# One program for the second layer's norm, routing and refinement, with three blocks of masks made inside the refinement

## The chip, the cores and the metric

The kernel runs on one core of a Trainium2 chip. The metric is the device time of one execution in microseconds. TensorE (PE) multiplies, ScalarE (ACT) evaluates functions and copies, VectorE (DVE) does elementwise work, GpSimd (POOL) helps, and SyncE (SP) starts transfers. Each runs its own instruction list in order and waits for the others by semaphores.

## The reference, cut to what matters

Two layers work on 2 x 1024 tokens of width 128. Only the last part, `_L1_ffn_ref`, is touched. It starts from a layernorm of the residual `x`:

```
logits = gelu(xf @ w_r1 + b_r1) @ w_r2 + b_r2          # 8 experts
top_p, top_i = top_k(softmax(logits), 2); top_p /= sum(top_p)
for _ in range(2):                                      # NUM_ITER
    ctx = concat(integrated, v)
    shared = inl(gelu(ctx @ w_s1 + b_s1) @ w_s2 + b_s2)
    routed = sum over the 2 picks c of top_p[c] * inl(gelu(ctx @ w1[i_c] + b1[i_c]) @ w2[i_c] + b2[i_c])
    x_next, v = sw * shared + (1 - sw) * routed
    integrated += sigmoid(gelu(x_next @ w_h1 + b_h1) @ w_h2 + b_h2) * (gelu(x_next @ w_f1 + b_f1) @ w_f2 + b_f2) * iw
# inl: alpha, beta, gate = sigmoid, softplus, sigmoid of the three thirds of the control;
#      v' = alpha*v - beta*(x - mu); x' = x + 0.1*gate*v'
```

## The kernel before

Tokens lie along the free dimension: `x` and `hn` are 128 features x 2048 tokens, in 4 blocks of 512 (`BLK`), or 16 tiles of 128. The kernel is a chain of programs. Each `with nc.Block()` gives every engine its list, and at its end all engines meet at a barrier. After the latent attention, `experts_of_layer1` runs these, one after the other:

- a program that starts the loads of the expert weights (`ew2`, `eb2_rows`), halves two biases, and lets POOL clear 85 used semaphores (`clear_stale`);
- `split_bias`: seven DVE instructions split the expert bias into bf16 parts (`eb2w`);
- `normalise`: center product, squares, means over 128 partitions, square root and reciprocal, spreading of the 2048 inverse norms (L189), and the product into `hn`;
- `route`: the router's two products (one `products` program each), the choice of two experts for each token (DVE, L2473 to L2506, with one Exp on ACT), the turn of the choice from tokens along partitions to tokens along the free dimension (`picks`, 27 rows), and the spreading of `picks` to `masks` and `mixw`: for each block 8 masks (2 picks x 4 pairs of experts) and 2 weights, 40 products in all, which DVE and ACT copy out of PSUM;
- `refine`: eight units `u` (4 blocks, twice). `hidden(u)` is 5 products with a Gelu each on two banks; `mask(u)` multiplies the hidden values with the masks on DVE; `control(u, comp, s)` makes part `comp` (1 beta, 2 gate, 0 alpha) for pick 0, pick 1 or the shared expert. For a pick that is one product with `eb2w` (L2658) and four with `ew2` (L2661), fp32, two passes each. `halt_*` are the products of the halting head. The order on each engine is written out by hand. `log_exp` changes ACT's table for the softplus, `hidden` changes it back.

`products` gives each step a PSUM bank in turn out of eight, and PE waits for the engine that took the step eight places earlier.

Of the kernel before, what the change touches and what calls it, by code (L numbers as in the profile page):

```python
# [5 lines left out]
F32 = mybir.dt.float32  # L6
# [6 lines left out]
D = 128  # L13
# [19 lines left out]
        "b_s2_0", "b_s2_1", "b_s2_2", "stat_eps"] + [f"eb1_{p}" for p in range(4)] + [f"part{i}" for i in range(3)] + ["eps_rms", "eps_ln"]  # L33
# [101 lines left out]


def normalise(k, tag, src, ncols, outs, groups=1, eps=1e-5, centre=None):


    nc = k.nc  # L140
    nb, nt = ncols // BLK, ncols // TILE
    width = nt * groups
    with ExitStack() as ctx:
        sq = k.sb(f"{tag}_sq", [128, ncols], ctx=ctx)
        ve = k.sb(f"{tag}_ve", [128, width], ctx=ctx)
        sd = k.sb(f"{tag}_sd", [128, width], ctx=ctx)
        r = k.sb(f"{tag}_r", [128, width], ctx=ctx)
        t = k.sb(f"{tag}_t", [128, width], ctx=ctx)

        rx = r if groups == 1 else k.sb(f"{tag}_rx", [128, width, HD], ctx=ctx)  # L150
        centred = k.sem(f"{tag}_centred")
        src_ready = k.sem(f"{tag}_src_ready")
        squared = k.sem(f"{tag}_squared")
        stat_done = k.sem(f"{tag}_stat_done")
        var_ready = k.sem(f"{tag}_var_ready")
        sd_ready = k.sem(f"{tag}_sd_ready")
        r_ready = k.sem(f"{tag}_r_ready")
        spread = k.sem(f"{tag}_spread")
        scaled = k.sem(f"{tag}_scaled")
        own = k.sem(f"{tag}_own")  # L160
        stat = k.bank[6][:, 0:width]
        mean = k.m("mean128") if groups == 1 else k.m("mean8")
        per = BLK // TILE
        with nc.Block() as block:
            @block.tensor
            def _(pe):
                if centre is not None:
                    for b in range(nb):
                        nc.tensor.matmul(k.bank[b][:, :], k.m("center"), centre[:, sl(b)], start=True, stop=True)\
                            .then_inc(centred, 1)  # L170
                for b in range(nb):
                    pe.wait_ge(squared, b + 1)
                    for j in range(b * per, (b + 1) * per):
                        last = nc.tensor.matmul(stat[:, j * groups:(j + 1) * groups], sq[:, sl(j, TILE)], mean,
                                                start=True, stop=True)
                last.then_inc(stat_done, 1)
                pe.wait_ge(r_ready, 1)
                for b in range(nb):
                    if b >= 2:
                        pe.wait_ge(scaled, (b - 1) * len(outs))  # L180
                    elif centre is not None:
                        pe.wait_ge(src_ready, nb)
                    for j in range(per):
                        jt = b * per + j
                        if groups == 1:
                            lhs = r[:, jt:jt + 1].to_broadcast([128, 128])
                        else:
                            lhs = rx[:, jt * groups:(jt + 1) * groups, :].rearrange("p g d -> p (g d)")
                        last = nc.tensor.matmul(k.bank[4 + b % 2][:, sl(j, TILE)], lhs, k.m("ident"),  # L189
                                                start=True, stop=True)  # L190
                    last.then_inc(spread, 1)

            @block.scalar
            def _(act):
                for b in range(nb):
                    if centre is not None:
                        act.wait_ge(src_ready, b + 1)
                    nc.scalar.activation(sq[:, sl(b)], src[:, sl(b)], ACT.Square).then_inc(squared, 1)
                act.wait_ge(var_ready, 1)
                nc.scalar.activation(sd[:, :], ve[:, :], ACT.Sqrt).then_inc(sd_ready, 1)  # L200

            @block.vector
            def _(dve):
                link = linker(dve, own)
                if centre is not None:
                    for b in range(nb):
                        dve.wait_ge(centred, b + 1)
                        nc.vector.tensor_copy(src[:, sl(b)], k.bank[b][:, :]).then_inc(src_ready, 1)
                dve.wait_ge(stat_done, 1)
                nc.vector.tensor_scalar_add(ve[:, :], stat, eps).then_inc(var_ready, 1)  # L210
                dve.wait_ge(sd_ready, 1)
                link(nc.vector.reciprocal(r[:, :], sd[:, :]))

                link(nc.vector.tensor_tensor(t[:, :], r[:, :], r[:, :], ALU.mult))
                link(nc.vector.tensor_tensor(t[:, :], t[:, :], ve[:, :], ALU.mult))
                link(nc.vector.tensor_scalar(t[:, :], t[:, :], -0.5, 1.5, ALU.mult, ALU.add))
# [2896 lines left out]
```

## Time and profile before

| | |
|---|---|
| median of 3 runs | 2122.79 us (2122.67 to 2124.22) |
| profiled execution | 2126.78 us, its span 2125.0 us |
| busy, share of the span | PE 84%, DVE 72%, ACT 65%, POOL 32% |
| share of the chain that ended last | PE 13% (of it L2661 7%), DVE 1%, ACT 1% |
| last part begins | about 1742.2 us into the span, the refinement at 1809.7 us |

Busy time is a share of the whole span, so it averages stages with different limits. The granted clock (PEclk) is a share of 2.4 GHz: 1.00 is 2.4 GHz and 0.50 is 1.2 GHz. In rows of the trace, `L12` is a line of the kernel, `xN` the number of instructions merged, and the bracket behind a row the idle time of the engine before it and what ended it. An fp32 product shows two matmuls. PEld is the loading of weights.

### The profile page before, as it was taken

Reading aid. Unit: us, or ns where it says so; the run is one execution under the profiler, and the core shown is the slowest. Engines: PE = TensorE matmul, PEld = TensorE weight load, DVE = VectorE, ACT = ScalarE, POOL = GpSimd, SP = SyncE. Lnnn points to the kernel's source line nnn. Section 1 sums busy time; section 2 is a strip of 40 time slices with the busy share of each in tenths; the row PEclk is TensorE's granted clock in tenths of the full one; section 3 lists DMA queues with packets and bytes.
Section 4 is the critical chain, followed back from the end, with each engine's and each line's share of the span. In section 5 each row is a group of like instructions: output and inputs, shape, how many; then the busy total and the mean of one; then the engine's idle time right before and its main releaser. Section 6 shows DMA issues by size and latency. Waiting matters only on the chain. (4 is left out here: it accounts for less than half of the span.)

```text
span 2125.0 us, 31609 instructions
## 1 busy us (share of the span) xinstructions
PE 1775.6 (84%) x10320; PEld 730.3 (34%) x10320; DVE 1534.3 (72%) x1538; ACT 1388.8 (65%) x2914; POOL 678.3 (32%) x384
## 2 busy tenths in 40 slices
PE   6799999997787666667666679989999977999996
PEld 1233333333333333333333234334444434333332
DVE  5788888844799999999999854456666625456446
ACT  2277777775899999999999724235555544344343
POOL 1000000001799999999999820010000000000000
PEclk8599999999688878887888799869999986999997
DMA  4111111001666665555555320412323100000000
GB/s 157 44 27 30 32 32 27 13 2 34 216 207 207 202 201 200 197 196 199 201 199 202 119 80 10 95 45 45 56 39 56 23 17 1 0 0 0 0 5 15
DMA packets 57886, 182.39 MB, mean 86 GB/s; under 512 B 8487, under 2 KB 11842, under 8 KB 56239
## 3 DMA queue, kind: packets, MB, share of 16 engines
q1 hardware_dynamic: 57487, 180.46, 28.0%
q8 instruction: 70, 1.15, 0.2%
q10 hardware_dynamic: 288, 0.45, 0.1%
q14 instruction: 41, 0.34, 0.1%
HBM read 160.60 MB, written 7.21 MB: 79 GB/s over the span
## 5 line engine op out<-in xcount | busy, mean ns | idle before, releaser
L648 DVE TENSOR_REDUCE attn_mx<-banks 128x1 f32<-128x1024 f32 (+7 forms) x512 | 501.5, 989 | 161.4 <-PE banks L455 102.2
L600 ACT ACTIVATE attn_probs<-banks 128x512 f32<-128x512 f32 (+3 forms) x896 | 446.5, 550 | 256.6 <-PE banks L485 151.6
L1722 POOL TENSOR_TENSOR hc<-st,ct 128x1024 f32<-128x1024 f32 x256 | 598.5, 2364 | 46.7 <-DVE st L1680 46.6
L1680 DVE TENSOR_TENSOR_SCAN st<-da,banks 128x1024 f32<-128x1024 f32 x256 | 566.6, 2269 | 19.7 <-DVE banks L1672 13.4
L1645 ACT ACTIVATE ut<-b_turned,x_now 128x128 f32<-128x128 f32 x1280 | 389.6, 387 | 3.1 <-PE banks L1538 1.4
L1637 ACT ACTIVATE da<-dt,a_now 128x1024 f32<-128x1024 f32 x256 | 284.1, 1136 | 10.6 <-DVE st L1680 8.9
L1538 PE MATMUL banks<-mats,ut 128*128 128x128 f32 x1280 | 234.5, 328 | 56.6 <-DVE st L1680 36.0
L505 PE MATMUL banks<-attn_probs,attn_vst 128*32 128x256 f32 (+3 forms) x3584 | 273.2, 376 | 4.1 <-ACT attn_osb L591 3.8
L485 PE MATMUL banks<-attn_qa,attn_ka 75*128 75x512 bf16 (+3 forms) x896 | 271.8, 372 | 4.2 <-DMA attn_qa<-attn_mrow 1.9
L1561 PE MATMUL banks<-hc,onecol 128*32 128x512 f32 x1024 | 178.9, 778 | 100.6 <-POOL onecol L1713 91.0
L1538 PEld LDWEIGHTS banks<-mats,ut 128*128 128x128 f32 x1280 | 183.1, 163 | 170.2 <-ACT ut L1645 101.2
L453 PE MATMUL banks<-attn_ka,attn_qa 64*128 64x512 bf16 (+3 forms) x512 | 198.9, 389 | 31.9 <-DVE attn_mx L648 27.2
L2661 PE MATMUL banks<-hid_m,ew 128*128 128x512 f32 x320 | 150.3, 613 | 0.0
L453 PE MATMUL banks<-attn_ku,attn_qu 64*128 64x512 bf16 (+3 forms) x384 | 145.3, 379 | 0.0
L1421 POOL MEMSET dr<- 1x2048 f32 x1 | 1.8, 1797 | 418.5 <-POOLq L355 418.5
L485 PEld LDWEIGHTS banks<-attn_qa,attn_ka 75*128 75x128 bf16 x896 | 80.8, 98 | 132.2 <-ACT attn_probs L600 56.9
L453 PEld LDWEIGHTS banks<-attn_ka,attn_qa 64*128 64x128 bf16 x512 | 47.8, 94 | 205.6 <-issue 130.4
L505 PEld LDWEIGHTS banks<-attn_probs,attn_vst 128*32 128x32 f32 x3584 | 73.4, 109 | 101.8 <-issue 90.8
L1551 PE MATMUL banks<-xparts,sel 96*128 96x512 bf16 x160 | 65.4, 501 | 44.7 <-DVE st L1680 43.4
L1672 DVE TENSOR_TENSOR banks<-bt,banks 128x1024 f32<-128x1024 f32 x80 | 96.6, 1207 | 1.7 <-PE banks L1551 1.7
L2661 PEld LDWEIGHTS banks<-hid_m,ew 128*128 128x128 f32 x320 | 58.4, 192 | 71.0 <-issue 71.0
L2845 DVE TENSOR_TENSOR beta<-beta,beta_raw 128x1536 f32<-128x1536 f32 x8 | 14.1, 1758 | 84.0 <-ACT beta L2773 84.0
(430 smaller groups left out, 1765.5 us busy)
## 6 DMA issues: line engine op xcount, KB each, us to landing
dt<-dt_rows SPq DMA_DIRECT2D x256, 512.0 KB, 4.1
attn_qa<-q_lin SPq DMA_DIRECT2D x144, 64.0 KB
attn_qu<-attn_qa SPq DMA_DIRECT2D x16, 512.0 KB, 4.2
attn_ka<-k_lin SPq DMA_DIRECT2D x72, 64.0 KB
moe_w<-in_moe_w SPq DMA_DIRECT2D x2, 2048.0 KB, 10.4
mats<-in_mats SPq DMA_DIRECT2D x1, 2876.5 KB, 15.2
attn_ku<-attn_ka SPq DMA_DIRECT2D x8, 256.0 KB, 5.0
q_lin<-qparts SPq DMA_DIRECT2D x6, 256.0 KB
```

Of the source, the lines that this page charges most:

```text
L453: ins = nc.tensor.matmul(out[:, lo:hi], lhs, rhs, start=True, stop=not diag)
L485: ins = nc.tensor.matmul(out[:, c0:BLK], ka[i % RING][0:KROWS, kj(j), sl(kt, TILE)], qa[i % RING][0:KROWS, j, qb * BLK + c0:(qb + 1) * BLK ...
L505: last = nc.tensor.matmul(out_acc[32 * j:32 * j + 32, cols], vstage[:, kt, kj(j), :], probs[(kt_slot + j // 2) % 4][:, j % 2, cols],  star ...
L600: nc.scalar.activation(probs[s % 4][:, jj, c0:BLK], scores_exp[jj][:, c0:BLK], ACT.Exp, scale=scale).then_inc(probs_ready, 1)
L648: nc.vector.reduce_max(mx[:, qt, j:j + 1], scores_max[n % 2][:, 0:w], AX.X)\
L1538: ins = nc.tensor.transpose(pair[:, i // 4, sl(i % 4, TILE)], buf[:, i, :], k.m("ident"))
L1561: last = nc.tensor.matmul(y_bank[h][32 * g:32 * g + 32, :], col[jp % 2][:, :], hc[(4 * jp + g) % 8][:, sl(h)], start=False, stop=False, sk ...
L1637: nc.scalar.activation(da[n % 4][:, :], dt[n % 4][:, :], ACT.Exp, scale=a_now[:, g, jp:jp + 1])\
L1645: nc.scalar.activation(ut[TURNED.index(n) % 2][:, i, :], b_turned[:, 8 * b + i, :], ACT.Copy, scale=x_now[:, i, g, jp:jp + 1]).then_inc(ut ...
L1680: nc.vector.tensor_tensor_scan(st[n % 4][:, :], da[n % 4][:, :], pair[:, :, :].rearrange("p h t -> p (h t)"), 0.0, ALU.mult, ALU.add).then ...
L1722: nc.gpsimd.tensor_tensor(hc[n % 8][:, :], st[n % 4][:, :], ct[:, b * SEQ:(b + 1) * SEQ], ALU.mult)\
L2661: last = nc.tensor.matmul(out[:, :], w2[:, p, comp * D:(comp + 1) * D], hid_m[u % 2][:, s, p, :], start=False, stop=p == PAIRS - 1)
```

## The change

All of that becomes one program, with one barrier before it and one behind it:

- The norm takes its guess from Ln and Exp (ACT, one table) and one refining step (DVE), squares are read from PSUM, and the kept copies of the centered values lie in buffers of the refinement.
- The router writes its four blocks to four row groups of one bank, so that one Gelu covers them. `hidden(0)` is issued around the logits: 2 of its 5 products before, 3 behind.
- The constants (`ident_b`, `sel`, `sel_w`, `half_b`, `hb2`) and the split bias are made on POOL, behind its clearing of semaphores (`tables` counts them: 4 before the first turn, 14 before the first control product).
- Only block 0 has its choice turned and its masks made ahead of the refinement, on six banks. Blocks 1 to 3 are 36 ring steps (per block 2 turns and 10 masks or weights), on banks 6 and 7 alone. 2 are issued ahead of the first control product, the other 34 between the control products of units 0 and 1, and ACT alone copies them out. Halting products, which use the same banks, wait for the last ring copy.

The pieces stand in this order: where the ring steps lie (`(u, comp, s)`: first step, count), PE's ring, PE's control product, PE's halting product of units 0 and 7, PE's start, ACT's start and unit, DVE's mask.

```
+    in_ring = {(0, 1, 0): (2, 4), (0, 1, 1): (6, 4), (0, 1, 2): (10, 4), (0, 2, 0): (14, 4), (0, 2, 1): (18, 4),
+               (0, 2, 2): (22, 4), (1, 1, 0): (26, 2), (1, 1, 1): (28, 2), (1, 1, 2): (30, 2), (1, 2, 0): (32, 2),
+               (1, 2, 1): (34, 2)}
...
+            def ring(first, count):
+                for n in range(first, first + count):
+                    b, r = 1 + n // RING, n % RING
+                    if n >= 2:
+                        pe.wait_ge(ring_copied, n - 1)
+                    if r == 2:
+                        pe.wait_ge(ring_copied, n)
+                    out = k.bank[6 + n % 2]
+                    ins = turn(out, b, r) if r < 2 else widen(out, b, r - 2)
+                    ins.then_inc(ring_made, 1)
...
                 for p in range(PAIRS):
                     last = nc.tensor.matmul(out[:, :], w2[:, p, comp * D:(comp + 1) * D], hid_m[u % 2][:, s, p, :],
                                             start=False, stop=p == PAIRS - 1)
-                last.then_inc(made, 1)
+                    if p == PAIRS - 1:
+                        last.then_inc(made, 1)
+                    if count == PAIRS:
+                        ring(first + p, 1)
+                    elif count and p % 2:
+                        ring(first + p // 2, 1)
...
+                else:
+                    pe.wait_ge(ring_copied, RINGS)
...
-            hidden(0)
+            normalise()
+            router()
+            hidden(0, 0, 2)
+            logits()
+            hidden(0, 2)
+            first_block()
+            ring(0, 2)
...
+            normalise()
+            router()
             hidden(0)
+            nc.scalar.preload_act_table_set("natural_log_exp_and_others")
+            act.wait_ge(diff_ready, 1)
+            nc.scalar.activation(best[:, :, 1], best[:, :, 1], ACT.Exp).then_inc(exps_ready, 1)
+            first_block()
+            ring(0, 2)
             for u in range(NU):
...
+                for s in (0, 1, SHARED):
+                    ring(*in_ring.get((u, 1, s), (0, 0)))
                 if u + 1 < NU:
                     hidden(u + 1)
-                gates(u, 0)
-                gates(u, 1)
+                for s in (0, 1):
+                    ring(*in_ring.get((u, 2, s), (0, 0)))
+                    gates(u, s)
...
             def mask(u):
+                if u == 0:
+                    dve.wait_ge(masks_dve, PAIRS + 1)
+                    dve.wait_ge(masks_act, PAIRS + 1)
+                elif u < NBLK:
+                    dve.wait_ge(ring_copied, RING * u)
```

On PE, the start of the refinement before: `hid_m` are the masked hidden values, `ew` the expert weights, `hn` the normalized input of `hidden`.

```order
L733 MATMUL banks_7<-picks,route_sel_w 128x512
L725 UNCONDITIONAL_BRANCH
L2626 UNCONDITIONAL_BRANCH
L2641 MATMUL banks_1<-hn,mats 128x512 x4
L2641 MATMUL banks_1<-hn,mats 64x512
L2658 MATMUL banks_3<-picks,eb2w 128x512
L2661 MATMUL banks_3<-hid_m,ew 128x512 x4
L2658 MATMUL banks_3<-picks,eb2w 128x512
L2661 MATMUL banks_3<-hid_m,ew 128x512 x4
L2654 MATMUL banks_5<-hid_s,mats 128x512
L2641 MATMUL banks_1<-hn,mats 128x512 x4
```

The same place in the changed kernel, from the last masks of block 0 on (`route_ident` with `route_tok` is a turn, `route_sel` with `picks` a mask, in its own numbering of lines):

```order
L2438 MATMUL banks_5<-picks,route_sel_w 128x512
L2430 MATMUL banks_7<-route_ident,route_tok 27x128 x8
L2502 MATMUL banks_3<-picks,eb2w 128x512
L2505 MATMUL banks_3<-hid_m,ew 128x512
L2438 MATMUL banks_7<-picks,route_sel 128x512
L2505 MATMUL banks_3<-hid_m,ew 128x512
L2438 MATMUL banks_7<-picks,route_sel 128x512
L2505 MATMUL banks_3<-hid_m,ew 128x512
L2438 MATMUL banks_7<-picks,route_sel 128x512
L2505 MATMUL banks_3<-hid_m,ew 128x512
L2438 MATMUL banks_7<-picks,route_sel 128x512
L2502 MATMUL banks_3<-picks,eb2w 128x512
```

The four `ew` products of a control product, which ran back to back, now have a bf16 mask product behind each of them.

On ACT, the first two units before (`mats` are the gates, `hid` the hidden values):

```order
L2740 ACT_TABLE_LOAD
L2740 ACTIVATE hid<-banks_1,cols 128x512 x4
L2743 ACTIVATE hid_s<-banks_1,cols 64x512
L2740 ACTIVATE hid<-banks_1,cols 128x512 x4
L2743 ACTIVATE hid_s<-banks_1,cols 64x512
L2754 ACTIVATE mats<-banks_5 128x512
L2754 ACTIVATE mats<-banks_3 128x512
```

The same stretch in the changed kernel, from the ring copies of block 1 on:

```order
L2617 CAST picks<-banks_7 27x512 x2
L2619 CAST masks<-banks_7 128x512 x4
L2619 COPY mixw<-banks_7 128x512
L2619 CAST masks<-banks_7 128x512 x4
L2619 COPY mixw<-banks_7 128x512
L2617 CAST picks<-banks_7 27x512 x2
L2631 ACT_TABLE_LOAD
L2631 ACTIVATE hid<-banks_1,cols 128x512 x4
L2634 ACTIVATE hid_s<-banks_1,cols 64x512
L2619 CAST masks<-banks_7 128x512 x4
```

ACT copies the ring's masks around the Gelus of unit 1, and these now stand behind a table load that was not there.

The routing's Exp on ACT before (`route_best` is the difference of the two best logits):

```order
L2510 ACT_TABLE_LOAD
L2510 ACTIVATE shared_w<-cols 128x1
L2512 ACT_TABLE_LOAD
L2512 ACTIVATE route_best<-route_best 128x16
L2513 CAST route_ident<-mats 128x128
```

And in the changed kernel (`hid` are the hidden values of unit 0):

```order
L2601 ACTIVATE shared_w<-cols 128x1
L2631 ACTIVATE hid<-banks_1,cols 128x512 x4
L2634 ACTIVATE hid_s<-banks_1,cols 64x512
L2687 ACT_TABLE_LOAD
L2689 ACTIVATE route_best<-route_best 128x16
L2605 CAST picks<-banks_7 27x512
```

The Exp and its table moved behind the five Gelus of `hidden(0)`.

## Rows read from the trace of the kernel before

**Rows 1.** Stages: us, busy and count of PE, PEld, DVE, ACT, POOL, PEclk, DMA, GB/s
```profile
1790.00:1809.70 19.70, 17.87 (x68) 7.74 (x65) 15.46 (x24) 13.34 (x24) 0.00 (x0) 0.59 0.00 1
...
1850.00:1880.00 30.00, 28.71 (x63) 10.05 (x63) 18.90 (x20) 14.76 (x17) 0.00 (x0) 1.00 0.00 0
```

**Rows 2.** Chain of waits in the refinement: start us, us, what
```profile
1818.42 0.37 PE banks L2658
1818.80 5.33 PE banks L2661 x8
...
1842.96 0.32 PE banks L2658
1843.27 3.63 PE banks L2661 x8
...
1851.90 1.07 PE banks L2641 x2
1853.07 1.28 ACT L2740
```

**Rows 3.** Timeline of PE: start us, us, what, idle before and its releaser
```profile
1752.67 6.50 PE L169 MATMUL banks<-x,mats 128*128 128x512 f32 x8 [11.23 <-PEq L2423]
1759.01 4.29 PE L174 MATMUL banks<-mats,ln_ffn_sq 128*128 128x1 f32 x32
1764.93 5.72 PE L189 MATMUL banks<-mats,ln_ffn_r 128*128 128x128 f32 x32 [1.64 <-DVE ln_ffn_r L218]
...
1776.32 4.65 PE L733 MATMUL banks<-mats,route_g 32*128 32x8 f32 x32 [1.02 <-PEq L725]
1789.35 3.44 PE L733 MATMUL banks<-route_ident,route_tok 128*27 128x128 bf16 x32 [8.38 <-PEq L2466]
```

**Rows 4.** Timeline of DVE
```profile
1741.48 0.69 DVE L705 TENSOR_TENSOR x<-x,banks 128x512 f32<-128x512 f32 x1 [0.21 <-PE banks L575]
...
1748.76 0.35 DVE L2428 CAST eb_hi<-eb_rows 27x384 bf16<-27x384 f32 x1 [6.04 <-PEq L2385]
...
1770.69 0.69 DVE L228 SCALAR_TENSOR_TENSOR hn<-ffn_hc,banks 128x512 f32<-128x512 f32 x1 [0.35 <-PE banks L189]
...
1781.61 0.28 DVE L2473 TENSOR_REDUCE route_best<-route_logits 128x16 f32<-128x128 f32 x1 [0.32 <-PEq L725]
...
1786.15 0.41 DVE L2490 CAST route_sel<-mats 27x512 bf16<-27x512 f32 x1
...
1786.80 0.16 DVE L2496 TENSOR_SCALAR route_prob<-route_best 128x16 f32<-128x16 f32 x1
...
1788.74 0.30 DVE L2506 TENSOR_TENSOR route_tok<-route_prob,route_tok 128x32 bf16<-128x32 f32 x1
...
1815.99 4.49 DVE L2827 TENSOR_TENSOR hid_m<-hid,masks 128x2048 f32<-128x2048 f32 x2 [7.32 <-ACT hid L2740]
```

**Rows 5.** Timeline of ACT
```profile
1790.39 0.57 ACT L2521 CAST picks<-banks 27x512 bf16<-27x512 f32 x1 [4.93 <-PE banks L733]
...
1799.01 0.59 ACT L2532 CAST masks<-banks 128x512 bf16<-128x512 f32 x1 [0.69 <-PE banks L733]
...
1870.87 1.28 ACT L2770 ACT_TABLE_LOAD   x1
1872.16 1.48 ACT L2771 ACTIVATE beta<-beta 128x1536 f32<-128x1536 f32 x1
```

**Rows 6.** Stretches of 2 us, columns as in rows 1
```profile
1744.00:1746.00 2.00, 0.00 (x0) 0.00 (x0) 0.00 (x0) 0.00 (x0) 0.00 (x0) 0.68 0.83 289
...
1798.00:1800.00 2.00, 2.00 (x6) 0.65 (x5) 2.00 (x4) 1.04 (x3) 0.00 (x0) 0.50 0.00 0
...
1822.00:1824.00 2.00, 2.00 (x4) 0.66 (x2) 0.00 (x0) 0.00 (x0) 0.00 (x0) 0.69 0.00 0
```

**Rows 7.** Timeline of the weight loads (PEld)
```profile
1846.83 0.09 PEld L2658 LDWEIGHTS banks<-picks,eb2w 27*128 27x128 bf16 x1 [0.76 <-issue]
```

**Rows 8.** Groups of POOL: count | busy us, mean ns
```profile
L1855 POOL TENSOR_SCALAR x<-x,cols 128x512 f32<-128x512 f32 x3 | 5.1, 1710 | 0.0
```

More of the change, by code:

```diff
@@ L2439, in route @@
-def route(k, ctx, masks, mixw, picks, shared_w):
-    nc = k.nc
-    g1 = k.sb("route_g1", [32, T], ctx=ctx)
+    masks = k.sb("masks", [128, 2, EXPERTS // 2, T], BF16, ctx)
+    mixw = k.sb("mixw", [128, 2, T], ctx=ctx)
+    picks = [k.sb(f"picks{c}", [PICK_ROWS, T], BF16, ctx) for c in range(2)]
+    shared_w = k.sb("shared_w", [128, 1], ctx=ctx)
+    routed_w = k.sb("routed_w", [128, 1], ctx=ctx)
+    w2 = k.sb("ew2", [128, EXPERTS // 2, 3 * D], ctx=ctx)
+    b2w = k.sb("eb2w", [PICK_ROWS, 3 * D], BF16, ctx)
@@ L2451, in route @@
     sel = k.sb("route_sel", [PICK_ROWS, EXPERTS, EH], BF16, ctx)
-    weight_rows = k.sb("route_weight_rows", [PICK_ROWS, 1], F32, ctx)
     sel_w = k.sb("route_sel_w", [PICK_ROWS, 128], BF16, ctx)
-    own = k.sem("route_own")
-    steps = [("act", one(k.m("w_r1"), k.hn[:, sl(b)], rows=slice(0, 32)),
-              lambda p, b=b: nc.scalar.activation(g1[:, sl(b)], p[0:32, :], ACT.Gelu, bias=k.c("b_r1", 32)))
-             for b in blocks(T)]
-    products(k, "route_p1", steps)
-    b_r2 = k.m("b_r2").unsqueeze(1).to_broadcast([128, NT, EXPERTS])
@@ L2541, in route @@
-    products(k, "route_spread", steps)
-def refine(k, ctx, xi, masks, mixw, picks, shared_w, w2, b2w, half_b, hb2, arrived, y):
-    nc = k.nc
     NU = 2 * NBLK
@@ new lines, in turn, with widen @@
+            def turn(out, b, c):
+                for j in range(4):
+                    last = nc.tensor.matmul(out[0:PICK_ROWS, sl(j, TILE)], tok[:, 4 * b + j, c, :], ident_b[:, :],
+                                            start=True, stop=True)
+                return last
+            def widen(out, b, m):
+                c, p = m // (PAIRS + 1), m % (PAIRS + 1)
+                lhs = sel_w[:, :] if p == PAIRS else sel[:, 2 * p:2 * p + 2, :].rearrange("r e m -> r (e m)")
+                return nc.tensor.matmul(out[:, :], lhs, picks[c][:, sl(b)], start=True, stop=True)
@@ L2746, in gates @@
             def gates(u, s):
+                if s == 0 and u == 0:
+                    act.wait_ge(tables, 5)
                 if s == 0 and u >= 2:
@@ L2806, in _ @@
                 gates(u, SHARED)
+                ring(*in_ring.get((u, 2, SHARED), (0, 0)))
                 if u >= 1:
@@ L2962, in _ @@
             sp.wait_ge(y_sent, 16 * NBLK)
+    k.free_stale()
 def build_program(nc, d, y):
```

475 lines of the change are left out of this document (221 added, 254 removed).

## Prediction

> **What bounds the kernel now.** I read the chain of waits first, then the stages, then the timelines of the engines. The chain shows the refinement as one unbroken row of TensorE (PE) pieces: from 1818.42 to 2070 us nearly every piece is PE's, the exception a table load of ScalarE (ACT) that PE waits for once per unit [rows 2]. In a stage of it PE is busy 28.71 of 30 us, at the full clock [rows 1]. There, every microsecond added to PE is added to the time. Between the last addition of the layer before (it ends at 1742.17) [rows 4] and the first control product at 1818.42 [rows 2] lie 76.25 us in which nobody is the bound. The engines work in turn: PE waits 11.23 us, then 8.38 us [rows 3], and DVE waits 6.04 us for the program in which POOL clears semaphores [rows 4]. In the mask stage PE is busy 17.87 of 19.70 us, but at a mean clock of 0.59 [rows 1]. So the change shortens a serial stage and lengthens one that PE fills.
>
> **The front, step by step.** I follow the new order from 1742.17 on.
> - Entry: 0.32, as after another barrier [rows 4].
> - Center: eight fp32 passes. They took 6.50, mostly at 1.2 GHz, after 11.23 us of idleness [rows 3]. Now PE was busy until just before, and the clock fell only within 1744 to 1746, when PE had been idle since before 1742 [rows 6]. So I take the full clock, half of the time: 3.4. The other end is 6.5.
> - Squares and copies lie beside PE. Means: 4.29 [rows 3].
> - Small chain: PE waited 1.64 for five DVE instructions and one of ACT [rows 3]. Now there are three and two: 1.35.
> - Spreading and last product: 1764.93 [rows 3] to 1771.38 [rows 4], 6.45.
> - Router, last block: two passes and the wait, 0.95. Its Gelu is hidden by two hidden products, 1.9 (one is 1.07 [rows 2]).
> - Logits: 4.65 [rows 3].
> - Choice of experts: DVE is at its wait for the Exp 4.5 after its start (1781.61 to 1786.15 [rows 4]), 4.75 with the additions. ACT's way there is longer: PE's three other hidden products, six passes of 0.81 (6.50/8 [rows 3]) since PE's clock sinks beside the logits' narrow products, 4.9; the last Gelu 0.85, the new table load 1.28 [rows 5], the Exp 0.3: 7.35. The later counts: 7.35. With the full clock it is 4.9.
> - Rest of the choice: 1786.80 to 1789.04 [rows 4], and one instruction more, 2.45. The constants that DVE made in between are POOL's now.
> - Turn and picks of one block: 1789.35 [rows 3] to 1790.96 (1790.39 + 0.57 [rows 5]), with a wait 1.7.
> - Ten masks: a turn of 128 columns takes 0.107 (3.44/32 [rows 3]), so 512 columns take 0.43 at the low clock that a wait of 8.38 leaves. 4.3, and the last copy 0.8 (0.59 [rows 5] and a wait).
> - First half of `mask(0)`: 4.49/2 [rows 4] and a wait, 2.3.
>
> Sum: 0.32 + 3.4 + 4.29 + 1.35 + 6.45 + 0.95 + 1.9 + 4.65 + 7.35 + 2.45 + 1.7 + 5.1 + 2.3 = 42.2. Against 76.25 this saves 34.0. It contains every barrier, the split of the bias, the 85 clearings and the 30 masks that moved.
>
> **POOL's tables.** They hide beside PE and DVE. Clearing took some 6 us [rows 4]. Of the 14 instructions behind it none is wider than a 128x512 TENSOR_SCALAR of 1.71 [rows 8], so the last ends before 1748.8 + 14 x 1.71 = 1772.7. It is needed at 1784.4. Cost 0. If each took twice that, PE would wait about 12 us. The DMA of the bias, first in its queue as before, landed before 1748.76.
>
> **What the refinement gains in length.** 34 ring steps go between PE's products.
> - A mask between fp32 products: a control product took 0.32 + 3.63 [rows 2], and eight uninterrupted passes would take 8 x 0.43 = 3.42. So the bf16 product in front costs 0.52: its weights 0.09, which PE does not load ahead [rows 7], 0.21 of columns, and about 0.2 for the fp32 weights behind it, now uncovered too. A mask inside a control product pays 0.52, one right ahead of the next bf16 product 0.31. Four control products get 3 x 0.52 + 0.31 = 1.87 each, four get 0.83: 10.8. Bounds for the 24 steps: 0.21 each if all loads are covered (5.0) and 0.86 if each waits for its ACT copy (20.6). I take the middle, since it is this very sequence.
> - Steps behind the shared product, where nothing covers ACT's copy of 0.59 and the wait behind it: four steps with two banks add 2.05 in the gate-free place, 2.5 where a gate's Tanh comes first, and two steps 0.6. Together 5.15.
> - ACT now holds the Exp table before the Gelus of unit 1, so PE stalls there too: 1.3, as at 1853.07 [rows 2].
> - The first halting product waits for the last ring copy: 0.8.
> - The first control product ran partly at 1.2 GHz, 5.33 against 3.63 [rows 2], until the clock rose within 1822 to 1824 [rows 6]. Now PE arrives cold, and the first four steps lie in it: 1.0 more.
>
> Sum 19.05. DVE and ACT have room: 18.90 and 14.76 busy of 30 [rows 1]. ACT gets 36 copies of 0.59, 21 us over units 0 and 1, where `log_exp` stands once in between: the step behind it waits for a copy that ends about 1.3 us before it is needed, so 0.
>
> Net: 34.0 - 19.05 = 14.9 less. The profiled execution took 2126.78 us (span 2125.0), 4.0 over the median. 2126.78 - 14.9 = 2111.9 there, and 2122.79 - 14.9 = 2107.9 as a median: **2108 us**.
>
> **Two rules of the Trainium skill.** A table load takes 1.28 and the next instruction follows 1.29 after its start [rows 5]. The Trainium skill, "ScalarE: Activation LUTs", section "What ACT_TABLE_LOAD costs", adds a drain and counts 2.66 us for a switch. By that the two new switches on the path cost 2.8 us more, and the kernel gains 12. The trace does not agree; the sum goes by the row.
> From 1798 to 1800 PE is busy 2.00 of 2.00 us with masks, and the clock is 0.50 [rows 6]. The Trainium skill, "TensorE: Matmul & The Clock Gate", section "Why this matters for your kernels", asks for a TensorE kept busy continuously to get the full clock. By busy time these masks would have had it; the trace does not agree for products of 27 rows. What that means inside the refinement is the fourth rival.
>
> **Rivals.**
> 1. *Quicker.* PE keeps 2.4 GHz in the hidden products (2.4 less), and loads for masks are half covered (3 less), the cold start costs nothing (1 less): 2101 us. For it: a clock of 1.00 in the refinement [rows 1]. Against: the load is uncovered each time [rows 7].
> 2. *The ring is bound by ACT.* ACT takes its list in order, and a ring copy behind Gelus, gates or `log_exp` holds both banks. At 0.86 a step the 24 steps cost 9.8 more: 2118 us. For it: two banks, one reader. Against: ACT is half idle [rows 1], and 0.9 us of products lie between steps.
> 3. *POOL is late*, slowed by DVE beside it. With 7 us of wait: 2115 us. Against: 11.7 us of slack even by the longest row.
> 4. *Slower: the clock.* Masks alone kept PE at 0.50 though busy [rows 6]. If masks between fp32 passes did that in units 0 and 1, the 47.6 us of PE's work from 1818.42 to 1866 would take up to 42 us more: 2122.8 - 14.9 + 42 = 2150 us. It outweighs the gain once 14.9 us of that work runs at half clock. Against: fp32 passes of 128 rows fill four fifths of the time, and `eb2w` products of 27 rows among them left the clock at 1.00 [rows 1].
>
> **Chances.** Forecast 0.57 (own range 2103 to 2113), quicker 0.15, ring bound by ACT 0.18, POOL late 0.04, clock 0.06. 0.2%, 4.2 us, is about what a measurement can tell from no change. The first four lie below 2118.5 nearly whole: faster 0.90. Within: 0.04, the tail of the ACT rival. Slower 0.06. The range 2100 to 2117 leaves out half of the second and third case and the clock.
>
> **What would show it.** The first control product starts 42 us after the last addition: between 40 and 46. The center at 0.43 a pass; DVE idle some 2.6 us ahead of its first `route_prob` instruction, with ACT's table load in that time. In the refinement, a mask every 1.4 us within a control product, none with a wait for ACT over 0.2 us; unit 1's Gelus behind a table load; PEclk 1.00 from the second control product on. From unit 2 on everything is as before. Wrong: PE idle inside control products (rival 2), 0.50 in the clock after 5 us (rival 4), or a first control product that waits for POOL.

## The result, and the profile after

| | before | after |
|---|---|---|
| median of 5 runs | 2124.22 us (2122.67 to 2126.94) | 2106.94 us (2102.26 to 2110.36) |
| profiled execution | 2126.78 us, span 2125.0 | 2109.03 us, span 2107.3 |
| last addition ends | 1742.17 | 1738.00 |
| first control product | 1818.42 | 1779.74 |
| first halting product | 1865.92 | 1851.44 |
| from there to the end | 259.08 | 255.86 |

The ratio is 0.9914, with a 95% interval of 0.9896 to 0.9932: faster by 17.3 us. The spans differ by 17.7, and the landmarks split that in four. The front (last addition to first control product) fell from 76.25 to 41.74, by 34.5. Units 0 and 1 grew from 47.50 to 71.70, by 24.2. The stretch behind them is 3.2 shorter with the same instructions, and the stages ahead of the last addition, also unchanged, are 4.2 shorter. So the change itself is worth 10.3 us in these two executions, less than the medians say.

The front on PE. Columns here and in all timelines: start, us, engine, line, operation, tile, count, and in brackets the idle time before it and what ended it.

```profile
1738.32 3.67 PE L2391 MATMUL banks<-x,mats 128*128 128x512 f32 x8 [1.04 <-PEq L259]
1741.83 4.75 PE L2397 MATMUL banks<-mats,hid 128*128 128x1 f32 x32
1748.12 6.79 PE L2406 MATMUL banks<-mats,route_inv 128*128 128x128 f32 x32 [1.55 <-DVE route_inv L2733]
1754.84 1.90 PE L2414 MATMUL banks<-hn,mats 128*32 128x512 f32 x8
1756.67 1.99 PE L2482 MATMUL banks<-hn,mats 128*128 128x512 f32 x4
1758.58 2.47 PE L2423 MATMUL banks<-mats,sum_a 32*128 32x8 f32 x32
1760.98 4.65 PE L2482 MATMUL banks<-hn,mats 128*128 128x512 f32 x6
1770.42 1.03 PE L2430 MATMUL banks<-route_ident,route_tok 128*27 128x128 bf16 x8 [4.79 <-DVE route_tok L2781]
...
1779.74 0.58 PE L2502 MATMUL banks<-picks,eb2w 27*128 27x512 bf16 x1 [1.33 <-issue]
```

The waits of 11.23 and 8.38 us [rows 3] are gone. The largest one left, 4.79, is the choice of experts. It holds the wait for the Exp, on DVE:

```profile
1767.91 0.15 DVE L2771 TENSOR_SCALAR routed_w<-shared_w 128x1 f32<-128x1 f32 x1 [1.96 <-ACT route_best L2689]
```

And on ACT, which spends 1.28 of it on the table [rows 5]:

```profile
1765.67 0.68 ACT L2634 ACTIVATE hid_s<-banks,cols 64x512 f32<-64x512 f32 x1 [0.32 <-PE banks L2482]
1766.37 1.28 ACT L2687 ACT_TABLE_LOAD   x1
1767.67 0.22 ACT L2689 ACTIVATE route_best<-route_best 128x16 f32<-128x16 f32 x1
```

Units 0 and 1 on PE: first the start, then a stretch at full clock, the end of the first half of unit 0, and the stall of unit 1.

```profile
1780.25 2.08 PE L2505 MATMUL banks<-hid_m,ew 128*128 128x512 f32 x2
1782.26 0.60 PE L2438 MATMUL banks<-picks,route_sel 27*128 27x512 bf16 x1
1782.79 2.08 PE L2505 MATMUL banks<-hid_m,ew 128*128 128x512 f32 x2
...
1795.69 1.12 PE L2505 MATMUL banks<-hid_m,ew 128*128 128x512 f32 x2
1796.74 0.39 PE L2438 MATMUL banks<-picks,route_sel 27*128 27x512 bf16 x1
1797.06 1.13 PE L2505 MATMUL banks<-hid_m,ew 128*128 128x512 f32 x2
...
1800.55 0.88 PE L2430 MATMUL banks<-route_ident,route_tok 128*27 128x128 bf16 x8 [0.46 <-ACT masks L2619]
1801.36 1.98 PE L2482 MATMUL banks<-hn,mats 128*128 128x512 f32 x4
1804.60 2.99 PE L2482 MATMUL banks<-hn,mats 128*128 128x512 f32 x6 [1.26 <-ACT hid L2631]
...
1851.44 1.02 PE L2522 MATMUL banks<-x_next,mats 128*32 128x512 f32 x2 [0.77 <-ACT mixw L2619]
```

Two fp32 passes and a mask take 2.54 us at the start (1780.25 to 1782.79) and 1.37 later (1795.69 to 1797.06). There is no wait in either: it is the clock. The stages show it (PE, PEld, DVE, ACT and POOL busy, PEclk, DMA share, GB/s):

```profile
1770.00:1780.00 10.00, 6.73 (x27) 2.93 (x27) 7.13 (x10) 4.56 (x8) 0.00 (x0) 0.50 0.00 0
1780.00:1794.00 14.00, 14.00 (x18) 3.52 (x18) 2.53 (x2) 2.86 (x5) 0.00 (x0) 0.50 0.01 1
1794.00:1796.00 2.00, 2.00 (x4) 0.39 (x3) 0.00 (x0) 0.28 (x2) 0.00 (x0) 0.68 0.00 0
1796.00:1822.00 26.00, 23.38 (x64) 6.80 (x63) 7.29 (x6) 15.75 (x27) 0.00 (x0) 1.00 0.00 0
1822.00:1826.00 4.00, 4.00 (x9) 1.37 (x8) 0.00 (x0) 3.94 (x5) 0.00 (x0) 0.57 0.00 0
1826.00:1851.00 25.00, 23.40 (x54) 7.54 (x53) 17.69 (x18) 11.67 (x18) 0.00 (x0) 1.00 0.00 1
```

PE is busy 14.00 of 14.00 us from 1780 on and still stands at 1.2 GHz. Before, the first control product began at the full clock (0.95 from 1818 to 1820), the clock fell for some 3.4 us and was back some 5 us after its start [rows 6]. Now PE arrives at 0.50, the rise takes 15 us, and the clock falls once more at 1822, again for some 3.4 us. In between, from 1796 to 1822, control products with the same masks inside run at 1.00.

The end differs by the clock too. Counted from the first halting product, PE's products start within 0.03 us of each other in both kernels up to 220.7 us. Of the 3.2 us, 3.1 arise in the next 13 (the next product with `halt_hid` starts at 2099.25 before and at 2081.65 after). Of the kernel before:

```profile
2086.00:2094.00 8.00, 7.38 (x8) 1.68 (x8) 4.79 (x6) 2.05 (x3) 0.00 (x0) 0.50 0.09 33
```

Of the changed kernel, the same place by its distance from the first halting product:

```profile
2072.00:2080.00 8.00, 7.88 (x14) 2.39 (x15) 6.06 (x7) 2.74 (x4) 0.00 (x0) 0.80 0.09 33
```

8 matmuls fit into these 8 us before and 14 after, about as the granted clocks 0.50 and 0.80 stand.

### The profile page after: what moved, and what is told of

It reads as the page before. It is cut to its first block and busy times, and to the rows that moved or that the text cites. A ratio compares the mean times of both kernels' runs of the same rounds, so it can differ in the third digit from the quotient of the medians.

```text
span 2107.3 us, 31537 instructions
## 1 busy us (share of the span) xinstructions
PE 1778.2 (84%) x10320; PEld 725.3 (34%) x10320; DVE 1518.9 (72%) x1509; ACT 1395.1 (66%) x2928; POOL 689.5 (33%) x398
## 5 line engine op out<-in xcount | busy, mean ns | idle before, releaser
L2505 PE MATMUL banks<-hid_m,ew 128*128 128x512 f32 x320 | 159.7, 635 | 0.0
```

What stands on the lines that cost most here:

```text
L2505: last = nc.tensor.matmul(out[:, :], w2[:, p, comp * D:(comp + 1) * D], hid_m[u % 2][:, s, p, :], start=False, stop=p == PAIRS - 1)
```

## The experiments

Two stretches of the profiled executions leave out what comes before and after the change: from the first center product to the first control product, and from there to the first halting product. Medians are of the timed runs, with their ratio to the kernel before on the same chip.

| run | center to control | control to halting | halting to end | median (profiled where not timed) | ratio |
|---|---|---|---|---|---|
| before | 65.75 | 47.50 | 259.08 | 2124.22 | |
| after | 41.42 | 71.70 | 255.86 | 2106.94 | 0.9914 |
| e1_again | 41.42 | 71.70 | 255.86 | 2106.8 | 0.9922 [0.9904, 0.9941] |
| e2_all_first | 54.03 | 48.62 | 256.07 | 2102.75 | 0.991 [0.9893, 0.9928] |
| e3_rows128 | 39.65 | 59.82 | 256.43 | 2095.12 | 0.9873 [0.9852, 0.9893] |
| e4_tanh | 36.55 | 66.29 | 255.83 | 2101.38 | 0.9907 [0.9886, 0.9928] |
| e5_before | 65.36 | 45.79 | 259.07 | (2125.27) | |
| e6_pairs | 37.26 | 67.14 | 258.22 | (2104.11) | |
| e7_padb | 36.71 | 56.95 | 251.62 | 2089.3 | 0.9857 [0.984, 0.9874] |
| e8_full | 38.62 | 56.99 | 239.30 | 2073.12 | 0.9778 [0.9763, 0.9793] |
| e9_full_tanh | 37.98 | 54.91 | 236.24 | 2074.44 | 0.9763 [0.9746, 0.978] |
| e10_full_tanh_all_first | 47.83 | 45.34 | 237.10 | 2073.17 | 0.9765 [0.9752, 0.9778] |
| e11_before_full | 59.10 | 42.52 | 237.02 | 2093.42 | 0.9852 [0.9832, 0.9872] |
| e12_full_again | 38.09 | 56.10 | 237.20 | 2075.65 | 0.9785 [0.9768, 0.9801] |

**The changed kernel again.** No edit.

> The changed kernel once more, as the base for the three kernels beside it. Its time should be 0.991 of before, within 0.3%, and it should move by up to 4 us from execution to execution, since the clock of TensorE (PE) stood at 1.2 GHz for 15 us at the start of the refinement in the first profile and where it rises depends on the moment. If the move comes from elsewhere, the length from the center product to the first control product (41.4 us) and from there to the first halting product (71.7 us) repeats within 1 us and the rest varies.

The stretches are those of the first profile to 0.01 us, and the clock rises at the same place. The whole is 2.1 less: between these two executions all of the difference lies upstream.

**All masks ahead of the refinement.** The program stays one, the ring goes; six banks, DVE and ACT copy.

```
-    in_ring = {(0, 1, 0): (2, 4), (0, 1, 1): (6, 4), ...}
+    in_ring = {}
+    STEPS = 2 * NBLK + WIDE * NBLK
...
+                for n in range(STEPS):
+                    out = k.bank[2 + n % 6]
+                    ins = turn(out, n // 2, n % 2) if n < 8 else widen(out, (n - 8) // WIDE, (n - 8) % WIDE)
```

> The changed kernel, but the masks of all four blocks are made ahead of the refinement, on six banks, copied by DVE and ACT in turn; no ring steps. Theory A (the gain is the merging of the programs, and the moved masks are a loss): the front grows by 6 turns of 0.43 and 30 masks of 0.43 at the low clock, about 15 us, from 41.4 to 57; the refinement up to the first halting product shrinks from 71.7 to about 50 (47.6 as before, 1.3 for the Gelu table, 1 to 2 of low clock); in all 5 to 8 us faster than the changed kernel. Theory B (the moved masks hide in the refinement): it is slower than the changed kernel by 5 us or more.

The front gains 12.6 us in length and units 0 and 1 lose 23.1: the moved masks cost more inside than ahead, as theory A had it. Over both, 102.65 against 113.12, 10.5 less where 5 to 8 were expected. The medians differ by 4.1 (2102.75 against 2106.8), and the intervals of their ratios overlap. PE arrives at 0.50 here too, and without masks between the products the clock is up 3.3 us after the first control product, not 15.

**Mask operands of 128 rows.** The 101 rows below the 27 are zero.

```
-    picks = [k.sb(f"picks{c}", [PICK_ROWS, T], BF16, ctx) for c in range(2)]
+    picks = [k.sb(f"picks{c}", [128, T], BF16, ctx) for c in range(2)]
-    sel = k.sb("route_sel", [PICK_ROWS, EXPERTS, EH], BF16, ctx)
+    sel = k.sb("route_sel", [128, EXPERTS, EH], BF16, ctx)
...
+            for n, tile in enumerate((picks[0][:, :], picks[1][:, :], sel[:, :, :], sel_w[:, :])):
+                nc.gpsimd.memset(tile, 0.0).then_inc(padded, 1)
+                pool.wait_ge(padded, n + 1)
```

> The changed kernel, but the operands of the mask products have 128 rows, of which 101 hold zeros: same columns, same number of products, more of PE's rows in use. Four memsets on POOL ahead of its tables, which are not waited for. Theory A (products of 27 rows hold the clock at 1.2 GHz, though PE counts as busy): the clock is at 2.4 GHz within 5 us of the first control product, and from there to the first halting product it takes 64 to 67 us in place of 71.7. Theory B (the clock stays low because PE arrives cold and waits between products): clock and length stay as they are, within 1 us.

Same instructions on PE, same number of columns, 11.9 us less from control to halting, where theory A expected 5 to 8. The row where the clock rises, of this kernel:

```profile
1780.00:1782.00 2.00, 2.00 (x4) 0.82 (x3) 0.65 (x1) 0.40 (x1) 0.00 (x0) 0.50 0.00 0
1782.00:1784.00 2.00, 2.00 (x5) 0.77 (x4) 0.00 (x0) 0.50 (x2) 0.00 (x0) 0.63 0.00 0
1784.00:1786.00 2.00, 2.00 (x7) 0.58 (x5) 0.38 (x1) 1.02 (x3) 0.00 (x0) 1.00 0.04 8
...
1814.00:1822.00 8.00, 8.00 (x21) 2.97 (x19) 3.14 (x3) 5.52 (x7) 0.00 (x0) 1.00 0.00 0
```

The clock is up 4 to 5 us after the first control product (1778.55) instead of 15, and the second dip is gone. And its timeline of PE at full clock:

```profile
1783.48 1.02 PE L2506 MATMUL banks<-hid_m,ew 128*128 128x512 f32 x2
1784.34 0.38 PE L2439 MATMUL banks<-picks,route_sel 128*128 128x512 bf16 x1
1784.56 1.02 PE L2506 MATMUL banks<-hid_m,ew 128*128 128x512 f32 x2
```

Two passes and a mask now take 1.08 (1783.48 to 1784.56) instead of 1.37. Two passes alone are 0.86, so a mask costs 0.22 instead of 0.51. 0.21 is its columns; what went is the loading of weights on both sides of it. The loads (PEld) show it. In the changed kernel each starts only with its product (the mask of 1796.74 and the pass of 1797.06 above):

```profile
1796.74 0.09 PEld L2438 LDWEIGHTS banks<-picks,route_sel 27*128 27x128 bf16 x1 [0.76 <-ACT masks L2619]
1797.06 0.30 PEld L2505 LDWEIGHTS banks<-hid_m,ew 128*128 128x128 f32 x2 [0.23 <-issue]
```

With 128 rows they start ahead of their products, the mask of 1784.34 and the pass of 1784.56:

```profile
1783.91 0.10 PEld L2439 LDWEIGHTS banks<-picks,route_sel 128*128 128x128 bf16 x1 [0.24 <-issue]
1784.34 0.41 PEld L2506 LDWEIGHTS banks<-hid_m,ew 128*128 128x128 f32 x2 [0.33 <-issue]
```

At the full clock a control product with four masks took 5.72 and 5.80 us and takes 4.81; one with two took 4.69 and 4.76 and takes 4.38. Over the eight of them that is about 5 of the 11.9 us by an estimate from these rows, and the clock the rest. The expectation had only the clock in it. The Trainium skill, "TensorE: Matmul & The Clock Gate", section "Step-by-step: what each phase is for", says that PE loads weights ahead of running products when row groups don't conflict or the load goes to the background weight buffer. Between products of 128 rows these rows agree with it; between 27 and 128 rows no load came ahead. The page names no such case.

**Tanh instead of Exp.** The weight of the pick comes from half the score by Tanh, in the table set of the Gelu, so both new table loads go.

```
-            nc.scalar.preload_act_table_set("natural_log_exp_and_others")
...
-            nc.scalar.activation(best[:, :, 1], best[:, :, 1], ACT.Exp).then_inc(exps_ready, 1)
+            nc.scalar.activation(best[:, :, 1], best[:, :, 1], ACT.Tanh, scale=0.5).then_inc(exps_ready, 1)
```

> The changed kernel, but the two probabilities come from a Tanh, which lies in the Gelu's table, in place of Exp and reciprocal; two table loads on ACT go. If these loads cost what the profile shows (1.28 each, no drain): DVE's wait of 1.96 in the choice shrinks to about 0.7, PE's stall of 1.26 in the hidden products of unit 1 goes, in all 2.5 to 3 us less. If the order of the Gelus was the cause and not the load, the first of the two stays. If a switch costs 2.66 as a page of the notes has it, 5 us less.

The two waits are gone, but 2.5 to 3 us were expected, and the stretches fall by 4.9 and 5.4 and the median by 5.4 (2101.38 against 2106.8). In this execution the clock rose 6.7 us after the first control product, not 15, and in front three hidden products took 2.99 us in place of 4.65 and the spreading 5.47 in place of 6.79. So part of it is where the clock happened to change, and the loads' own share is not separated.

**The kernel before once more.**

> The kernel before once more, for a second profile. If the stretch from the last addition of the layer before to the first halting product (123.8 us in the first profile) repeats within 1 us, the change's own gain is the difference to 113.4 us; the 4 us by which the changed kernel reached its norm earlier and the 3 us by which its end was shorter should be seen to vary between executions of the same code.

It repeats to 0.4 us in the front, 1.7 in units 0 and 1 and 0.01 in the end. The expectation missed twice. From the last addition to the first halting product it took 121.65 us, 2.1 less than in the first profile: the clock stayed at 1.00 from 1818 on. So the change's own gain is 8.2 to 10.3 us. And the end did not vary: it was 259.08 and 259.07 in the kernel before, and 255.8 to 256.4 in five of the six runs from the changed one whose tiles behind unit 1 are unchanged (258.22 in e6_pairs). Whether the change has a part in where the clock falls at the end stays open.

**Ring steps in pairs.**

```
-                    if count == PAIRS:
-                        ring(first + p, 1)
-                    elif count and p % 2:
-                        ring(first + p // 2, 1)
+                    if count == PAIRS and p % 2:
+                        ring(first + p - 1, 2)
+                    elif count and p == PAIRS - 1:
+                        ring(first, 2)
```

> The changed kernel, but the ring steps in a control product stand two and two (behind its second and fourth ew product) in place of one behind each, and in unit 1 both behind the fourth. Same work. Theory (each return from a 27-row product to 128-row products leaves a weight load uncovered, 0.3 us): 8 returns fewer in unit 0 and 4 fewer in unit 1, so 3.6 us less from the first control to the first halting product at the full clock. Rival (a mask's price is its own and the place does not matter): within 1 us of the changed kernel, or longer if ACT does not copy two masks in time.

At full clock a pair takes 0.53 (1803.01 to 1803.54) and 0.20 more on the passes beside it, 0.73 against 2 x 0.51 apart: 0.29 less for a return, as expected. The whole can't be compared with the 3.6 expected. It fell by 4.6 to 67.14, but the clock stood at half for 9 us in place of 15 at the start, and again for 6 at 1814 in place of 3.4.

**The bias product `eb2w` of 128 rows as well** (on top of e3): `b2w` and the rows of `picks` that it reads.

```
-                nc.tensor.matmul(out[:, :], b2w[:, comp * D:(comp + 1) * D], picks[s][0:PICK_ROWS, cols(u)], start=True,
+                nc.tensor.matmul(out[:, :], b2w[:, comp * D:(comp + 1) * D], picks[s][:, cols(u)], start=True,
```

> As the kernel with 128-row mask products, and the product with eb2w in front of each pick's control product has 128 rows too (101 of them zeros), all 40 of them. Theory (27 rows leave the weight load behind the product uncovered, 0.3 us each time): 40 x 0.3 = 12 us less than with 128-row masks alone, most of it behind the first halting product, where that length falls from 256.4 to about 248. Rival (what uncovers the load is the change between bf16 and fp32, and the gain with 128-row masks was the clock): no change.

The end fell by 4.8 us, where 8 were expected, and the median by 5.8, where 12 were (taken on two chips; against the kernel before on the same chip it is 3.4). The direction is the theory's, the size half of it. Loads beside products of 64 and 32 rows stayed uncovered; those are the next edit.

**Every product of the refinement 128 by 128** (on top of e7): weights taken 128 columns wide where 32 or 64 were used, `hid_s` and `halt_hid` with zero rows.

```
-                        out, lx, lv = hidden_bank[n % 2][0:EH, :], k.m("w_s1", lo=0, n=EH), k.m("w_s1", lo=EH, n=EH)
+                        out, lx, lv = hidden_bank[n % 2][:, :], k.m("w_s1", lo=0, n=128), k.m("w_s1", lo=EH, n=128)
...
-                nc.tensor.matmul(halt_bank(u, 0)[0:32, :], k.m("w_h1"), xn[:, :], start=True, stop=True)\
+                nc.tensor.matmul(halt_bank(u, 0)[:, :], k.m("w_h1", n=128), xn[:, :], start=True, stop=True)\
```

> As the last one, and all products of the refinement are full: the shared expert's hidden values (64 rows) and the halting head's (32) are padded with rows of zeros, and weights of 64 and 32 columns are taken 128 wide, with rows of the result that nobody reads. Theory (PE loads weights ahead only between products of the same full size, and each change of size costs about 0.2 us): 12 changes in a unit, in all 10 to 15 us less than with the eb2w product padded alone. Rival (waits on other engines uncover these loads): no change, or slower, since wider weight loads take longer (0.19 against 0.14 for 32 columns).

The end falls by 12.3 more, and the median by 16.2, where 10 to 15 were expected. A control product and its neighbours in the changed kernel:

```profile
1859.51 1.12 PE L2535 MATMUL banks<-halt_hid,mats 32*128 32x512 f32 x2
1860.47 0.38 PE L2502 MATMUL banks<-picks,eb2w 27*128 27x512 bf16 x1
1860.77 3.70 PE L2505 MATMUL banks<-hid_m,ew 128*128 128x512 f32 x8
1864.31 1.88 PE L2544 MATMUL banks<-ref_hid,mats 128*128 128x512 f32 x4
```

And with full tiles:

```profile
1838.86 1.02 PE L2536 MATMUL banks<-halt_hid,mats 128*128 128x512 f32 x2
1839.72 0.38 PE L2503 MATMUL banks<-picks,eb2w 128*128 128x512 bf16 x1
1839.93 3.60 PE L2506 MATMUL banks<-hid_m,ew 128*128 128x512 f32 x8
1843.37 1.88 PE L2545 MATMUL banks<-ref_hid,mats 128*128 128x512 f32 x4
```

From the halting product to `ref_hid` 4.80 became 4.51, though the full tiles hold up to nearly five times as many rows.

**Full tiles with Tanh, and the same with all masks ahead.** The edits are those of e4_tanh and e2_all_first on e8_full.

> Edit: the kernel of e8_full (every product of the refinement 128 by 128, spare rows and columns zero) with Tanh of half the score instead of Exp and its reciprocal, so that ScalarE never leaves the Gelu table set. Theory A (the two table loads stand on the path: 1.28 us ahead of the Exp while DVE idles, and about 1.3 us at the first unit behind it, in both units of e8_full a PE wait of 1.28): 2.5 to 4 us less than e8_full, so about 2069 to 2070 us. Theory B (e4's gain of 10 us between first centre product and halting was mostly the phase of TensorE's clock, which the padded rows have already lifted, and the loads were partly hidden): under 1 us less, 2072 to 2073.

> Edit: e9_full_tanh with all 24 masks of blocks 1 to 3 made ahead of the refinement again, on six banks, none inside the control products. Theory A (a mask inside a control product now costs 0.22 us between full tiles, 24 of them 5.3 us and about 1.2 us of waits at the ends of units, against 12.6 us that e2_all_first spent ahead of the refinement): 6 us slower than e9_full_tanh, about 2075 us, with some 12.6 us more from first centre to first control product and some 6.5 less from there to halting. Theory B (the masks were better ahead, as in e2_all_first, whatever the tile size): 2 to 4 us faster than e9_full_tanh, 2065 to 2067.

The Tanh missed: the medians show nothing (2074.44 against 2073.12 and 2075.65). The front is 0.1 to 0.6 shorter, units 0 and 1 are 1.2 to 2.1. In e8_full DVE never waits for the Exp. PE's hidden products take 3.03 at full clock instead of 4.65, and DVE is later by itself, since POOL now clears the padding first and works on `eb2w` into DVE's choice. DVE in e8_full:

```profile
1757.97 0.55 DVE L2756 SCALAR_TENSOR_TENSOR route_t<-route_t,mats 128x128 f32<-128x128 f32 x1
...
1759.21 1.06 DVE L2761 SCALAR_TENSOR_TENSOR route_logits<-route_t,route_logits 128x128 f32<-128x128 f32 x1
```

POOL in e8_full:

```profile
1757.76 1.28 POOL L2964 TENSOR_SCALAR alpha<-alpha,cols 27x384 f32<-27x384 f32 x1
1759.13 0.98 POOL L2965 TENSOR_TENSOR eb2w<-alpha 27x384 bf16<-27x384 f32 x1
```

Both DVE instructions took 0.29 in the changed kernel, with POOL done; the second ends at 1760.27, just behind POOL's second at 1760.11. The Trainium skill, "SBUF — State Buffer", section "Who interferes with whom", says of DVE's two-port modes that whichever of DVE and GpSimd issues first keeps the shared ports for its whole instruction, and that the other is blocked. Taken for this instruction too, the second pair agrees with it, with 0.77 us. The first does not: DVE ended at 1758.52, POOL's instruction beside it at 1759.04.

The masks ahead were to be 6 us slower, or 2 to 4 faster by theory B, and are neither: 9.85 longer in front, 9.57 shorter behind, and a median of 2073.17 against 2074.44. Its mask stage runs at full clock from 1772 on, where that of before had a mean of 0.59 [rows 1] and that of e2_all_first stood at 0.50 from 1780 to 1788 with PE busy throughout. Three stretches of e10:

```profile
1776.00:1778.00 2.00, 2.00 (x8) 0.45 (x8) 2.00 (x5) 1.95 (x5) 0.00 (x0) 1.00 0.00 0
...
1782.00:1784.00 2.00, 0.04 (x1) 0.00 (x0) 1.97 (x3) 0.66 (x2) 0.00 (x0) 1.00 0.00 0
...
1786.00:1788.00 2.00, 2.00 (x4) 0.87 (x4) 1.71 (x1) 0.00 (x0) 0.00 (x0) 0.50 0.00 0
```

PE then waits for DVE's first `mask(0)` and enters the refinement at 0.50; the clock is back 5.7 us after the first control product.

**The kernel before with full tiles, and e8_full once more beside it.** DVE clears the padding in the first program, where it waited for POOL. The rest is e8_full's edit.

> Edit: the kernel before, with the zero rows and the 128 columns of e8_full and nothing else (the buffers are cleared by DVE in the first program, where it waits some 6 us for POOL). It tells how much of the gain of e8_full over the kernel before is the change's and how much the tiles'. Theory A (the change gains in front and loses by its small masks between full tiles; with full tiles it keeps more of its gain): from halting on 16.6 us less, as between the changed kernel and e8_full; units 0 and 1 about 3.3 less, as between e2_all_first and e10; the mask stage 0 to 4 less; 2097 to 2101 us, so that the change with full tiles is worth some 25 us instead of 17. Theory B (the tiles' gain is the same with and without the change, the moved masks lose nothing by their shape): 31 us less than before wherever the masks stand, about 2090, and the change stays at 17.

> The kernel of e8_full once more, on the same chip as e11_before_full, since e8_full and e9_full_tanh were compared over two calls. Both theories: 2073 us within 3, from first control product to halting 57.0 us and from there to the end 239.3, both within 0.5 if TensorE's clock changes at the same place.

The kernel before gains 30 us too. The median of 2093.42 lies nearer to B's 2090 than to A's 2097 to 2101. From first turn to first control product it took 24.12 us (1789.74 to 1813.86) instead of 29.07 and 30.38 (e5_before), more than the 0 to 4 of theory A; units 0 and 1 fell by 3.3 to 5.0, the end by 22.1, where 16.6 was expected. Two stages of it with full tiles, after the first masks:

```profile
1790.00:1800.00 10.00, 8.87 (x56) 4.81 (x54) 8.40 (x14) 7.70 (x15) 0.00 (x0) 0.88 0.01 2
1800.00:1810.00 10.00, 7.75 (x24) 2.42 (x23) 6.36 (x11) 7.75 (x14) 0.00 (x0) 1.00 0.00 1
```

Between last addition and halting the change is worth 17.6 us with full tiles (112.13, that is 1744.25 to 1856.38, against 94.51, 1740.09 to 1834.60) and 8.2 to 10.3 without. By the medians it is 17.8 with and 17.3 without; these ratios are uncertain by some 4 us each, so that the profiles' 7 to 9 us more is not confirmed by the timed runs.

e12_full_again differs from e8_full by 0.9 us from control to halting and by 2.1 in the end, more than the 0.5 expected. The clock came up some 3 us after the first control product instead of 4.6, and the rest of it was not followed.

## Why the prediction was right, and where it was not

**Total and sign: right, the total by luck.** 2108 forecast, 2106.94 measured. The sum was less right than that: net 14.9 forecast, 10.3 in the two profiles (8.2 against e5_before), and 7.4 us that the sum did not contain made up for it. 3.2 lie in the last stretch, nearly all of it by the clock (0.50 against 0.80 for 8 us). The other 4.2 come ahead of the change and vary from run to run. 2.7 of them are there 49 us into the span already. The product that starts there starts between 48.1 and 51.5 in the kernels made from the changed one and between 48.4 and 50.8 in the three of before, so this part may well be chance. As for all 4.2, the last addition ended between 1735.8 and 1741.6 in the kernels made from the changed one and at 1742.17, 1742.78 and 1744.25 in the three of before. Whether the rest is more than chance stays open.

**The front: 42.2 forecast, 41.74 measured.** The terms of the sum, forecast then measured:
- right to 0.2: entry 0.32 and 0.32; center 3.4 and 3.51 (the full clock was the right choice); small chain 1.35 and 1.54; hidden products 1.9 and 1.91; rest of the choice 2.45 and 2.51; turn and picks 1.7 and 1.79; ten masks 5.1 and 5.05; `mask(0)` 2.3 and 2.48.
- means 4.29 and 4.75, spreading 6.45 and 6.72: the clock fell during them.
- router 0.95 and 1.83. The sum counted the last block alone. But PE spreads all inverse norms before it issues the router, so its eight passes come after the spreading together.
- logits 4.65 and 2.73, the term most wrong. The sum took the old duration. In four row groups the 32 passes take 0.075 us each (1758.58 to 1760.98); in one they took about 0.11 at full clock (1.69 us busy for 16 from 1776 to 1778). The rest of the difference is the clock, 0.71 from 1778 to 1780 before. The grouping was not tried alone.
- Exp path 7.35 and 6.60. DVE's wait was forecast at 2.6 and is 1.96.

The misses have opposite signs: means, spreading and router took 1.6 us more than forecast, logits and Exp path 2.7 less. That the sum came out within 0.5 us is in part luck. POOL was done at 1755.58, 24 us early: cost 0, as forecast.

**The refinement: 19.05 forecast, 24.2 measured.** The load terms hold: the eight control products with masks grew by about 10.4 at the full clock, where 10.8 was forecast. A mask inside a control product was put at 0.52 and took 0.51 (1.37 less 0.86). The steps behind the shared product were 5.15 and are 4.5 (1799.49 to 1801.36, 1820.10 to 1822.23 and 1834.44 to 1834.97). The table load was 1.3 and is 1.26, the halting wait 0.8 and 0.77. No other product waits for ACT, so the second rival had no part.

The step that failed is the last term of that sum, the cold clock at 1.0. Six pairs of passes with their mask took 2.31 to 2.54 instead of 1.28 to 1.37, 6.8 more together, two `eb2w` products 0.2 more each, and the dip at 1822 put 3.61 in place of 1.92 on four passes with their mask: 8.9, less the 1.7 that the kernel before pays too, is 7.2. 10.4 + 4.5 + 1.3 + 0.8 + 7.2 = 24.2, as measured. "PEclk 1.00 from the second control product on" was wrong: it was 1.00 from the third on, and not for good. This is the fourth rival in a small size, and the prediction's own sign for it, 0.50 after 5 us, came true. The argument against it, `eb2w` products that left the clock at 1.00 [rows 1], did not carry over to the new sequence as long as PE started from 0.50; once up, the clock stayed up from 1796 to 1822, through control products with the same masks, unit 1's hidden products and two waits.

e3_rows128 shows the cause by its edit: with zero rows, same columns and same order, the clock rises after 4 to 5 us. That PE arrives cold is not enough of a cause, since e2_all_first arrives cold too and rises after 3.3. Over all profiles that start the refinement at or near 0.50, the rise took 15, 15, 9 and 6.7 us with 27-row masks inside (the changed kernel twice, e6_pairs, e4_tanh) and 3 to 6 without them (e2_all_first and all with 128-row masks). What sets the time within a group is not shown.

**What the profile could have told.** The placement of the masks and the size of their tile act together. From first center to halting:

| | masks inside | masks ahead |
|---|---|---|
| 27 rows | 113.12 | 102.65 |
| full tiles, Tanh | 92.89 | 93.17 |

With small tiles the ring loses 10.5 us in these profiles (4 by the medians) against masks ahead in the same program, with full tiles nothing. The evidence was there: the mask stage at 0.50 with PE full [rows 6] for the clock, and the load that was not ahead [rows 7] for the price of a mask. The prediction had priced the second rightly, but no zero rows against it.

The best versions, e8_full and its two variants with Tanh, lie at 2073 to 2076 us, 2.2% to 2.4% below the kernel before, and can't be told apart.

## What to carry to other kernels

Look at the height and width of the products, not only at their columns: where a PE-bound stage mixes small with full tiles, zero rows and unused columns up to 128 cost PE nothing here and took 12 to 34 us out of the kernels that they were tried in. Clearing the rows took POOL some 7 us in e8_full, off the path but for 1.0 us on DVE. Ahead of moving work "beside" PE's products, ask at which clock the stage will then run; PE's busy share doesn't tell. And split a result by landmarks before believing that its sum was right: here 7 of 17 us came from stages that had not been changed.

## What the runs showed of the hardware that was not expected

- A stream of fp32 products with a 27-row bf16 product behind every two passes that started at 1.2 GHz stayed there for 15 us with PE busy 14.00 of 14.00 (6.7 and 9 in two variants); with 128 rows for 3 to 5 us. Once it had risen, the clock stayed at 1.00 from 1796 to 1822 with the same masks between the products.
- Weights were loaded ahead of their product between tiles of 128 rows (1783.91 for 1784.34), and for 27 rows behind 32 (1860.04 for 1860.47), but not between 128 and 27 rows (1796.74 for both) nor for 27 behind 64 (1820.09 for 1820.10). Among fp32 products of 128 rows, a bf16 product of 512 columns takes 0.22 with 128 rows and 0.51 with 27; an fp32 product of 32 or 64 rows 0.96 to 1.06 (1859.51 to 1860.47, 1798.43 to 1799.49) instead of 0.86 (1838.86 to 1839.72).
- Passes of 8 columns with 32 rows took about 0.11 us each in one row group and 0.075 in four, both near full clock.
- Two of DVE's SCALAR_TENSOR_TENSOR took 0.26 and 0.77 us longer beside POOL's work.
